# Nine chunks of the batch-weight product as three f16 products, with the splits on Pool

## The chip, the cores and the metric

The kernel runs on one NeuronCore of one Trainium2 chip. The metric is the device time of one execution in microseconds (us); lower is better.

## The reference, cut to what matters

A gated cross-attention block and a gated FFN stand one after the other, on x of 4 batches x 1024 rows x 256 columns, with a context of 154 rows per batch.

```
h   = layernorm(x)                                   # per row of 256
Sim = (h@w1)[:, :, None] + (ctx@w2)[:, None, :] + einsum(h*w3, ctx) + b_sim
A   = softmax(Sim, axis=2);  hq = A @ ctx
hc  = sum_i softmax(max_j Sim)_i * h_i               # one row per batch
out = concat([h, hq, h*hq, h*hc]) @ W_qv + b_qv      # W_qv: 1024 x 256
x1  = x + tanh(g_xattn) * out
y   = layernorm(x1), rounded to 16-bit integers by its largest value
up, gate = y @ Wup.T, y @ Wgate.T                    # 256 -> 768, weights in 4 bits
o   = silu-like product of gate and up, re-rounded at each step by its largest value
result = x1 + tanh(g_ffn) * (o @ Wdown.T)            # 768 -> 256
```

The first and last of the four blocks of `W_qv` are folded: `h @ W0 + (h*hc) @ W3 = h @ (W0 + hc*W3)`. The bracket is the batch weights, `we` in the kernel, one 256x256 matrix per batch. The change is about this product alone.

## The kernel before

The rows are tiled to 16 chunks of 256 (two tiles of 128 rows each), four chunks to a batch: `B = 4`, `NP = 4`, `N = 16`. Every engine has a program of its own, and they meet at semaphores only. In the attention stage each of them runs a loop over a step number `m`, with the order of the work inside a step written out by hand; `b, s = m // NP, m % NP`. Chunk n is normed and turned in step n, scored in step n + 1, and projected in step n + `LAG`, with `LAG = 7`.

On TensorE a step m is: `project(m - 7)`, `turn_h(m)`, `score(m - 1)`, `turn_a(m - 2)`, `attend(m - 3)`, `turn_y(m - 8)`. `project(n)` adds, for each of the two tiles, three pairs of f32 matmuls 128x256 into one PSUM tile: attended rows times W1 (L591), row products times W2 (L593), and rows times batch weights (L597). For the first chunk of a batch the work is parted, since `we` is not there yet: `project_first(b)` does the first two groups (L616, L618) in step 4b + 7, and `project_rest(b)` the third (L628) at that step's end. Between them stand `batch_cols(b)` (L663, L664), which turns the weighted row sum of the batch into a column, and `attend`.

The row sum comes over several engines: DVE's `batch_max` and `batch_shift` and ScalarE's `batch_exp` give a weight per row (`eb`); then Pool's `row_weigh` (L426, L433) and `row_add` (L439 to L443) weigh and sum the rows; `batch_cols` is TensorE's; DVE's `summary` (L1305 to L1313) makes `we` from it.

Pool does, in each step and in this order: `bias_x` for two chunks (in steps with s = 0 or 3; L451), `row_weigh` (s = 1), `y_std(m - 7)` (L397, L399: powers for the second layer norm), `row_add` (s = 2), `row_std(m + 3)` (L392: powers for the first), and parts of the rounding of the FFN weights (L413, L419). In step 16 and 17 the last batch's `row_weigh` and `row_add` come ahead of `y_std`. `row_std` waits for `vp_done`, the end of `stats` on DVE (L1184).

DVE does in step m, as far as it matters here: `attended(m - 4)` (L1231), `norm_x(m + 1)` while m < 7 (L1192), `scored(m - 1)` (L1215), `batch_max`, `stats(m + 3)`, `normed(m - 1)` (L1223), and later `residual(m - 7)` (L1239).

`partition_all_reduce` is a Pool instruction that reduces a column over the 128 partitions. In the kernel before only `over_all` (L488) uses it, four times, in the FFN stage. The projection weights `wv` come in by one DMA (L342) and are used as they are, in f32. The FFN stage follows: `hidden` (L774, L779) makes gate and up, `down` (L809) the last product, both as three f16 products (high x high, high x low, low x high).

Of the kernel before, what the change touches and what calls it, by code (L numbers as in the profile page):

```python
# [62 lines left out]
COLS = 320  # L63
W_SCALE = 2.0 ** 11


def build(nc, x, ctx, g_xattn, g_ffn, w_sim, b_sim, w_qv, b_qv, w_gate, w_up, w_down, out):
# [92 lines left out]
    cx = [cx01[:, 0], cx01[:, 1], cx23[:, 0], cx23[:, 1]]  # L160
    aT = place(a, "aT", [JP, 3, 2, PT], F32)

    a = copy_of(r_wd)
# [31 lines left out]
    c_g3, c_pid = col(3), col()  # L195
    c_bs = c_g3[:, 2:3]
    c_sm, c_sa, c_pw, c_wt, c_dn = col(), col(), col(), col(), col(3)
    c_loc, c_all = col(5), col(5)
# [18 lines left out]
    with ExitStack() as stack:  # L217
        def sem(name):
            return stack.enter_context(nc.semaphore(name))
# [29 lines left out]
        wchain, wall_rdy, wdiag_rdy, wm_ps, wri_rdy, wq_rdy, wqi_rdy, wqf_rdy, wn_rdy, wt_ps, wth_rdy, wt_rdy = map(  # L249
            sem, ("wchain", "wall_rdy", "wdiag_rdy", "wm_ps", "wri_rdy", "wq_rdy", "wqi_rdy", "wqf_rdy", "wn_rdy", "wt_ps", "wth_rdy", "wt_rdy"))  # L250
        ydiag_rdy, ym_ps = sem("ydiag_rdy"), sem("ym_ps")
        l_f_ps, l_xc_rdy, l_x1_rdy, l_bn_done, l_mv_done, l_vp_done, l_rstd_rdy, l_y_rdy, l_yT_ps = map(
# [44 lines left out]
        TURN_AT = {19: (0, 1, 2), 20: (3, 4, 5)}  # L297
        L = N - 1
        w_banks = [hT_bank, s_bank, a_bank]

# [84 lines left out]
        def _(pool):  # L385
# [59 lines left out]
            def bias_x(n):  # L445
# [5 lines left out]
                pool.tensor_tensor(x_, x_, txb[:].unsqueeze(1).broadcast_to([P, 2, D]), ALU.add).then_inc(xb_rdy, 1)  # L451

            pool.wait_ge(mhalf_rdy, 1)
            for n in range(1, NP):
                row_std(n)
            for m in range(N + LAG):
                b, s = m // NP, m % NP
                if s == 3 and 4 <= m < N + 4:
                    for n in range(2):
                        bias_x(m - 5 + n)  # L460
                if s == 0 and 4 <= m < N + 4:
                    for n in range(2):
                        bias_x(m - 4 + n)
                if s == 1 and 1 <= b < B or m == N:
                    row_weigh(b - 1)
                    row_pair(b - 1)
                if m == N + 1:
                    row_add(b - 1)
                for i in range(3):
                    if m == NORMS_AT[i] and i > 0:  # L470
                        weight_n(i)
                if LAG <= m < L + LAG:
                    y_std(m - LAG)
                if s == 2 and 1 <= b < B:
                    row_add(b - 1)
                if 1 <= m and m + 3 < N:
                    row_std(m + 3)
                for i in range(3):
                    if m in (SCALES_AT[i] + 1, SCALES_AT[i] + 2):
                        weight_q(i, m - SCALES_AT[i] - 1)  # L480
                    if m == NORMS_AT[i] and i == 0:
                        weight_n(i)
# [38 lines left out]
        def _(pe):  # L521
# [61 lines left out]
            def project(n, largest_of=None):  # L583
# [3 lines left out]
                for t in range(2):  # L587
# [6 lines left out]
                    if s == 0:  # L594
                        pe.wait_ge(we_rdy, b + 1)
                    for d in range(KD):
                        mm = pe.matmul(o_, hT[:, par, d, q], we[:, par, d, :], start=False, stop=d == KD - 1)  # L597
                    if t == 0 and largest_of is not None:
# [6 lines left out]
            def project_first(b):  # L605
# [3 lines left out]
                if b == 0:  # L609
                    pe.wait_ge(wqv_in, 16)  # L610
                ge(pe, x1_rdy, n - 1)
# [552 lines left out]
        def _(dve):  # L1164
# [68 lines left out]
            def residual(n):  # L1233

                g = 2 * n
                dve.wait_ge(f_ps, n + 1)
                dve.wait_ge(xb_rdy, n + 1)
                x_ = xa[:, g:g + 2, :]
                dve.scalar_tensor_tensor(x_, f_bank[n % 2].rearrange("p (t d) -> p t d", t=2), c_tx, x_,  # L1239
                                         ALU.mult, ALU.add).then_inc(x1_rdy, 1)  # L1240
# [13 lines left out]
            def last_y():  # L1254
# [4 lines left out]
                def last_stats(t):  # L1259
                    x_ = xa[:, 2 * L + t, :]  # L1260
                    dve.wait_ge(l_f_ps, t + 1)
                    i_ = dve.scalar_tensor_tensor(x_, last_f(t), c_tx, x_, ALU.mult, ALU.add)
                    i_.then_inc(l_x1_rdy if t == 0 else x1_rdy, 1)
# [39 lines left out]
            def summary(b):  # L1303
# [6 lines left out]
                if b == 0:  # L1310
                    dve.wait_ge(wqv_in, 16)
                for d in range(KD):
# [27 lines left out]
            def weight_unit(m):  # L1340

                dve.wait_ge(wm_ps, m + 1)
                dve.tensor_reduce(c_sa, s_bank[:, 3 * P:4 * P], AX.X, ALU.max).then_inc(wall_rdy, 1)
                dve.wait_ge(wall_rdy, m + 1)
                ulink(WU * m, dve.tensor_scalar(c_pw.bitcast(I32), c_sa.bitcast(I32), 0x7F800000, None, ALU.bitwise_and))
                ulink(WU * m + 1, dve.reciprocal(c_wt, c_pw))
                dve.tensor_scalar(c_dn[:, m:m + 1], c_pw, 1.0 / W_SCALE, None, ALU.mult)
                ulink(WU * m + 2, dve.tensor_scalar(wsc[:, m % 2], wsc[:, m % 2], c_wt, W_SCALE, ALU.mult, ALU.mult))

# [56 lines left out]
            for m in range(3, N + LAG - 1):  # L1406
# [38 lines left out]
                if s == 3 and b == 1:  # L1445
                    summary(b - 1)
                for i in range(3):
                    if m == SCALES_AT[i]:
# [255 lines left out]
```

## Time and profile before

| | |
|---|---|
| median of 3 runs | 438.53 us (437.5 to 438.99) |
| the profiled execution, its own time | 438.24 us |
| its span in the trace | 436.3 us |
| TensorE (PE) busy | 424.8 us, 97% of the span |
| DVE, ScalarE (ACT), Pool busy | 334.5, 295.3, 120.4 us |
| attention stage | up to about 172 us |
| first matmul of the FFN stage (L774) | 177.51 us |
| granted TensorE clock | 1.00 |

The page's second part shows the span in 40 slices of 10.9 us each, with the busy share in tenths:

```profile
PE   6899999999999999999999999999999999999997
DVE  6885778577573776864446799999899888997784
ACT  4886567568646443943335899994698888977750
POOL 1267545474769541040000213442000000000000
PEclk9999999999999999999999999999999999999999
DMA  7950002000200201100000000000000001343442
```

TensorE is full from about the third slice to the end. From its sixth part, on the projection weights (source, queue, KB, median us from issue to landing):

```profile
wv<-in_L_xattn_W_qv SPq DMA_DIRECT2D x1, 1024.0 KB, 8.2
```

An f32 matmul appears as two records, each with its own weight load. A row of the order of time has start, length, engine, line, operation, output and input; in brackets stands how long the engine had idled before, and who released it.

### The profile page before, as it was taken

The numbers are of one execution on the slowest core, as the hardware profiler recorded it, in microseconds if no ns is written. First come the engines' busy times: TensorE is split into PE (matmuls) and PEld (weight loads), VectorE is DVE, ScalarE is ACT, GpSimd is POOL, SyncE is SP. The second block draws the span as 40 slices with busy tenths as digits, with TensorE's granted clock in tenths as the row PEclk, the third lists the DMA queues.
The fourth block names the chain that finished last, engine by engine and source line by source line (L and its number), as shares of the span: only waits on it lengthen the run. The fifth ranks groups of instructions, "written<-read, shape, count | busy, mean of one in ns | idle before, by whom it ended". The sixth has DMA issues, their size and how long they took to land.

```text
span 436.3 us, 6912 instructions
## 1 busy us (share of the span) xinstructions
PE 424.8 (97%) x2424; PEld 293.6 (67%) x2424; DVE 334.5 (77%) x647; ACT 295.3 (68%) x404; POOL 120.4 (28%) x129
## 2 busy tenths in 40 slices
PE   6899999999999999999999999999999999999997
PEld 5788899999988987444444444444444444888886
DVE  6885778577573776864446799999899888997784
ACT  4886567568646443943335899994698888977750
POOL 1267545474769541040000213442000000000000
PEclk9999999999999999999999999999999999999999
DMA  7950002000200201100000000000000001343442
GB/s 241 326 192 2 1 2 97 2 1 24 75 2 0 98 0 37 61 0 0 0 0 2 0 0 1 0 0 2 0 0 0 0 0 54 116 121 123 144 144 74
DMA packets 20674, 21.14 MB, mean 48 GB/s; under 512 B 826, under 2 KB 20393, under 8 KB 20649
## 3 DMA queue, kind: packets, MB, share of 16 engines
q1 hardware_dynamic: 20628, 20.82, 15.3%
q8 instruction: 14, 0.23, 0.2%
q14 instruction: 12, 0.09, 0.1%
q10 hardware_dynamic: 20, 0.00, 0.0%
HBM read 12.43 MB, written 8.39 MB: 48 GB/s over the span
## 4 chain that ended last, share of the span: by engine, by line
PE 75%; DVE 14%; ACT 6%; issue 4%; POOL 0%; DVEq 0%; ACTq 0%
PE ps L774 17%; PE ps L809 13%; PE ps L779 9%; PE ps L579 5%; PE ps L591 5%; PE ps L597 5%; PE ps L593 5%; DVE cols L1525 5%; PE ps L560 3%; DVE hid L1541 2%; ACT hid L1083 2%; PE ps L569 1%; PE ps L636 1%; PE ps L546 1%; PE ps L628 1%
## 5 line engine op out<-in xcount | busy, mean ns | idle before, releaser
L774 PE MATMUL ps<-xh,wuh 128*128 128x512 f16 x192 | 72.8, 379 | 1.0 <-DVE gq L1565 1.0
L774 PE MATMUL ps<-xh,wul 128*128 128x512 f16 x192 | 72.8, 379 | 0.0
L779 PE MATMUL ps<-xl,wuh 128*128 128x512 f16 x192 | 57.1, 379 | 0.0
L1504 DVE TENSOR_REDUCE cols<-hid x10 | 22.9, 2286 | 24.4 <-ACT hid L1059 24.4
L809 PE MATMUL ps<-wdh,oh 128*128 128x256 f16 x168 | 37.4, 273 | 0.0
L809 PE MATMUL ps<-wdl,oh 128*128 128x256 f16 x168 | 37.4, 273 | 0.0
L1059 ACT ACTIVATE hid<-ps 128x2048 f32 x10 | 18.8, 1875 | 27.5 <-PE ps L779 27.5
L774 PE MATMUL ps<-xh,wgh 128*128 128x512 f16 x96 | 36.4, 379 | 0.1
L774 PE MATMUL ps<-xh,wgl 128*128 128x512 f16 x96 | 36.4, 379 | 0.0
L774 PEld LDWEIGHTS ps<-xh,wuh 128*128 (+1 forms) x192 | 18.8, 98 | 24.3 <-issue 2.0
L779 PEld LDWEIGHTS ps<-xl,wuh 128*128 (+1 forms) x192 | 18.8, 98 | 22.7
L774 PEld LDWEIGHTS ps<-xh,wul 128*128 (+1 forms) x192 | 18.8, 98 | 22.4
L488 POOL PARTITION_ALL_REDUCE cols<-cols x4 | 1.5, 364 | 115.7 <-DVE cols L1463 109.8
L579 PE MATMUL ps<-aT,cx 77*128 77x256 f32 x128 | 30.6, 382 | 0.0
L1146 ACT ACTIVATE oq<-hid,cols 128x1536 int16 (+1 forms) x15 | 23.6, 1572 | 10.1 <-DVE ol L1627 10.1
L921 ACT ACTIVATE yb<-xa,cols 128x256 f32<-128x256 f32 x30 | 16.3, 592 | 20.3 <-POOL cols L399 20.3
L1118 ACT ACTIVATE au<-ps,cols 128x512 int16<-128x512 f32 x40 | 25.8, 691 | 5.6 <-PE ps L779 5.6
L1541 DVE CUSTOM_DVE_ANT_0 hid<-ag,sq 128x2048 f32<-128x2048 int16 x12 | 29.1, 2424 | 0.2
L1525 DVE TENSOR_REDUCE cols<-ps 128x1 f32<-128x2048 f32 x12 | 27.4, 2285 | 1.6 <-PE ps L779 1.6
L779 PE MATMUL ps<-xl,wgh 128*128 128x512 f16 x96 | 28.6, 379 | 0.0
L591 PE MATMUL ps<-wv,hqT 128*128 128x256 f32 x104 | 26.7, 379 | 0.0
L597 PE MATMUL ps<-we,hT 128*128 128x256 f32 x104 | 26.7, 379 | 0.0
(235 smaller groups left out, 1025.7 us busy)
## 6 DMA issues: line engine op xcount, KB each, us to landing
x_scratch<-xa SPq DMA_DIRECT2D x4, 1024.0 KB, 4.4
xo<-x_scratch SPq DMA_DIRECT2D x16, 256.0 KB, 2.9
out_dram<-xo SPq DMA_DIRECT2D x15, 256.0 KB, 2.6
xa<-in_x SPq DMA_DIRECT2D x3, 1024.0 KB, 12.6
xa<-in_x SPq DMA_DIRECT2D x4, 256.0 KB, 4.5
wv<-in_L_xattn_W_qv SPq DMA_DIRECT2D x1, 1024.0 KB, 8.2
wr<-in_L_ffn_w_gate SPq DMA_DIRECT2D x1, 768.0 KB, 10.1
wr<-in_L_ffn_w_up SPq DMA_DIRECT2D x1, 768.0 KB, 11.5
```

The costliest lines, as they stand in the source:

```text
L579: mm = pe.matmul(hq_bank[:, d * PT:(d + 1) * PT], cx[b][0:JP, k, d * P:(d + 1) * P], aT[0:JP, n % 3, k, :], start=k == 0, stop=k == 1)
L591: pe.matmul(o_, hqT[:, par, d, q], wv[:, KD + d, :], start=d == 0, stop=False)
L593: pe.matmul(o_, prT[:, par, d, q], wv[:, 2 * KD + d, :], start=False, stop=False)
L597: mm = pe.matmul(o_, hT[:, par, d, q], we[:, par, d, :], start=False, stop=d == KD - 1)
L774: pe.matmul(ps[hf][:, q, :], w_[:, d, ds(k * P, P)], xh[:, d, n], start=d == 0 and w_ is wh, stop=False)
L779: mm = pe.matmul(ps[hf][:, q, :], wh[:, d, ds(k * P, P)], xl[:, d, n], start=False, stop=d == KD - 1)
L809: mm = pe.matmul(down_ps(par)[:, t], o_[:, par, k, q], w_[:, k, :], start=not low and k == 0 and w_ is wdh, stop=low and k == KF - 1)
L1118: a_ = act.activation(au[:, hf, bank_of(q)], ps[hf][:, q, :], ACT.Abs, scale=c_cu)
L1146: act.activation(oq[:, par], hid[:, :, ds(c * CD, CD)], ACT.Copy, scale=c_co).then_inc(oqa_rdy, 1)
L1504: dve.tensor_reduce(gmx[:, ds(k * 2 + hf, 1)], unit(hid, k, hf), AX.X, ALU.max, apply_absolute_value=True).then_inc(gm_done, 1)
L1525: dve.tensor_reduce(umx[:, u:u + 1], ps_half(u % 2), AX.X, ALU.max, apply_absolute_value=True).then_inc(half_free[u % 2], 1)
L1541: dve.tensor_tensor_reduce(half_of(hid, u), ag[:, u % 2, :], sq[u % 2][:], 1.0, 0.0, ALU.mult, ALU.max, pmx[:, u:u + 1]).then_inc(p_rdy, 1)
```

## The change

For the nine chunks 1, 2, 3, 5, 6, 7, 9, 10 and 11 (`SPLIT`) the group of L597 is no longer two f32 matmuls a tile but six f16 matmuls: high rows x high weights, high x low, low x high, for each of the two halves of the contraction. The chunks 0, 4, 8 (`project_rest`) and the last batch stay in f32.

Pool makes the f16 parts: `split_h(i)` casts the turned rows of a chunk to f16 and subtracts the cast from them, at the start of step n + 6; `split_weights(b)` does the same for `we`, in the steps with s = 3.

For the low parts to stay in f16's range, the projection weights are first scaled by a power of two: at step 3 DVE takes their largest absolute value per partition (`all_weights_largest`), at step 4 Pool reduces it over the partitions (`all_weights_max`, a `partition_all_reduce`) and DVE makes the scale and its inverse (`all_weights_unit`), at step 5 Pool multiplies all 128x2048 values in place (`all_weights_scaled`). The semaphore counts of another chain of DVE move by one set of three for it. What used `wv` waits for the scaling: `project_first(0)` and `summary(0)`. The residual takes the gate times the inverse scale (`c_txs`) in place of the gate (`c_tx`). The f16 tiles lie in memory that the FFN's up weights take later.

```diff
--- before.py
+++ after.py
@@ -62,6 +62,7 @@
 LN_EPS = 1e-5
 COLS = 320
 W_SCALE = 2.0 ** 11
+V_SCALE = 2.0 ** 10


 def build(nc, x, ctx, g_xattn, g_ffn, w_sim, b_sim, w_qv, b_qv, w_gate, w_up, w_down, out):
@@ -159,6 +160,11 @@
     cx23 = place(copy_of(r_wg), "cx23", [JP, 2, 2, D], F32)
     cx = [cx01[:, 0], cx01[:, 1], cx23[:, 0], cx23[:, 1]]
     aT = place(a, "aT", [JP, 3, 2, PT], F32)
+    a = copy_of(r_wu)
+    hTh = place(a, "hTh", [P, 2, KD, PT], F16)
+    hTl = place(a, "hTl", [P, 2, KD, PT], F16)
+    weh = place(a, "weh", [P, KD, D], F16)
+    wel = place(a, "wel", [P, KD, D], F16)

     a = copy_of(r_wd)
     cbi = place(a, "cbi", [P, 2, J], F32)
...
@@ -296,6 +304,7 @@
         TURNS = [(0, 0), (0, 1), (0, 2), (1, 0), (1, 1), (1, 2), (2, 0), (2, 1), (2, 2)]
         TURN_AT = {19: (0, 1, 2), 20: (3, 4, 5)}
         L = N - 1
+        SPLIT = [n for n in range(N - NP) if n % NP > 0]
         w_banks = [hT_bank, s_bank, a_bank]

         def w_part(m, q, low):
@@ -450,11 +459,47 @@
                 x_ = xa[:, 2 * n:2 * n + 2, :]
                 pool.tensor_tensor(x_, x_, txb[:].unsqueeze(1).broadcast_to([P, 2, D]), ALU.add).then_inc(xb_rdy, 1)

+            def split_h(i):
+
+                n = SPLIT[i]
+                b, s, par = place_of(n)
+                pool.wait_ge(pr_rdy, n + 1)
+                if i > 1:
+                    pool.wait_ge(f_ps, SPLIT[i - 2] + 1)
+                seen = hT[:, par, :, s * PT:(s + 1) * PT]
+                pool.tensor_copy(hTh[:, i % 2], seen).then_inc(hhl_rdy, 1)
+                pool.wait_ge(hhl_rdy, 2 * i + 1)
+                pool.tensor_tensor(hTl[:, i % 2], seen, hTh[:, i % 2], ALU.subtract).then_inc(hhl_rdy, 1)
+
+            def split_weights(b):
+
+                pool.wait_ge(we_rdy, b + 1)
+                ge(pool, f_ps, b * NP)
+                pool.tensor_copy(weh[:], we[:, b % 2]).then_inc(wvs_rdy, 1)
+                pool.wait_ge(wvs_rdy, 2 * b + 3)
+                pool.tensor_tensor(wel[:], we[:, b % 2], weh[:], ALU.subtract).then_inc(wvs_rdy, 1)
+
+            def all_weights_max():
+
+                pool.wait_ge(vunit_rdy, 1)
+                pool.partition_all_reduce(c_va, c_vg, P, RMAX).then_inc(wvs_rdy, 1)
+
+            def all_weights_scaled():
+
+                pool.wait_ge(vunit_rdy, 3)
+                pool.tensor_scalar(wv[:], wv[:], c_vs, 1.0, ALU.mult, ALU.mult).then_inc(wvs_rdy, 1)
+
             pool.wait_ge(mhalf_rdy, 1)
             for n in range(1, NP):
                 row_std(n)
             for m in range(N + LAG):
                 b, s = m // NP, m % NP
+                if m - LAG + 1 in SPLIT:
+                    split_h(SPLIT.index(m - LAG + 1))
+                if m == 5:
+                    all_weights_scaled()
+                if s == 3 and LAG <= m < N:
+                    split_weights(b - 1)
                 if s == 3 and 4 <= m < N + 4:
                     for n in range(2):
                         bias_x(m - 5 + n)
@@ -475,6 +520,8 @@
                     row_add(b - 1)
                 if 1 <= m and m + 3 < N:
                     row_std(m + 3)
+                if m == 4:
+                    all_weights_max()
                 for i in range(3):
                     if m in (SCALES_AT[i] + 1, SCALES_AT[i] + 2):
                         weight_q(i, m - SCALES_AT[i] - 1)
@@ -593,8 +640,18 @@
                         pe.matmul(o_, prT[:, par, d, q], wv[:, 2 * KD + d, :], start=False, stop=False)
                     if s == 0:
                         pe.wait_ge(we_rdy, b + 1)
-                    for d in range(KD):
-                        mm = pe.matmul(o_, hT[:, par, d, q], we[:, par, d, :], start=False, stop=d == KD - 1)
+                    if n in SPLIT:
+                        i = SPLIT.index(n)
+                        pe.wait_ge(hhl_rdy, 2 * i + 2)
+                        pe.wait_ge(wvs_rdy, 2 * b + 4)
+                        for d in range(KD):
+                            qt = slice(t * P, (t + 1) * P)
+                            pe.matmul(o_, hTh[:, i % 2, d, qt], weh[:, d, :], start=False, stop=False)
+                            pe.matmul(o_, hTh[:, i % 2, d, qt], wel[:, d, :], start=False, stop=False)
+                            mm = pe.matmul(o_, hTl[:, i % 2, d, qt], weh[:, d, :], start=False, stop=d == KD - 1)
+                    else:
+                        for d in range(KD):
+                            mm = pe.matmul(o_, hT[:, par, d, q], we[:, par, d, :], start=False, stop=d == KD - 1)
                     if t == 0 and largest_of is not None:
                         batch_max(largest_of)
                     if n == L:
@@ -607,7 +664,7 @@
                 n, par = b * NP, b % 2
                 pe.wait_ge(pr_rdy, n + 1)
                 if b == 0:
-                    pe.wait_ge(wqv_in, 16)
+                    pe.wait_ge(wvs_rdy, 2)
                 ge(pe, x1_rdy, n - 1)
                 for t in range(2):
                     q = slice(t * P, (t + 1) * P)
@@ -1235,8 +1292,10 @@
                 g = 2 * n
                 dve.wait_ge(f_ps, n + 1)
                 dve.wait_ge(xb_rdy, n + 1)
+                if n == 0:
+                    dve.wait_ge(vunit_rdy, 3)
                 x_ = xa[:, g:g + 2, :]
-                dve.scalar_tensor_tensor(x_, f_bank[n % 2].rearrange("p (t d) -> p t d", t=2), c_tx, x_,
+                dve.scalar_tensor_tensor(x_, f_bank[n % 2].rearrange("p (t d) -> p t d", t=2), c_txs, x_,
                                          ALU.mult, ALU.add).then_inc(x1_rdy, 1)
                 dve.wait_ge(x1_rdy, n + 1)
                 for t in range(2):
@@ -1259,7 +1318,7 @@
                 def last_stats(t):
                     x_ = xa[:, 2 * L + t, :]
                     dve.wait_ge(l_f_ps, t + 1)
-                    i_ = dve.scalar_tensor_tensor(x_, last_f(t), c_tx, x_, ALU.mult, ALU.add)
+                    i_ = dve.scalar_tensor_tensor(x_, last_f(t), c_txs, x_, ALU.mult, ALU.add)
                     i_.then_inc(l_x1_rdy if t == 0 else x1_rdy, 1)
                     dve.wait_ge(l_x1_rdy if t == 0 else x1_rdy, 1 if t == 0 else N)
                     dve.bn_stats(st[:, t, :], x_).then_inc(l_bn_done, 1)
@@ -1308,7 +1367,7 @@
                 dve.wait_ge(hc_rdy, b + 1)
                 ge(dve, f_ps, NP * (b - 1))
                 if b == 0:
-                    dve.wait_ge(wqv_in, 16)
+                    dve.wait_ge(wvs_rdy, 2)
                 for d in range(KD):
                     i_ = dve.scalar_tensor_tensor(we[:, b % 2, d, :], wv[:, 3 * KD + d, :], c_hc[:, d:d + 1], wv[:, d, :],
                                                   ALU.mult, ALU.add)
@@ -1342,10 +1401,24 @@
                 dve.wait_ge(wm_ps, m + 1)
                 dve.tensor_reduce(c_sa, s_bank[:, 3 * P:4 * P], AX.X, ALU.max).then_inc(wall_rdy, 1)
                 dve.wait_ge(wall_rdy, m + 1)
...
+
+            def all_weights_largest():
+
+                dve.wait_ge(wqv_in, 16)
+                ulink(0, dve.tensor_reduce(c_vl, wv[:].rearrange("p k n -> p (k n)"), AX.X, ALU.max, apply_absolute_value=True))
+                dve.tensor_scalar(c_vg, c_vl, EPS, None, ALU.max).then_inc(vunit_rdy, 1)
+
+            def all_weights_unit():
+
+                dve.wait_ge(wvs_rdy, 1)
+                ulink(1, dve.tensor_scalar(c_vp.bitcast(I32), c_va.bitcast(I32), 0x7F800000, None, ALU.bitwise_and))
+                ulink(2, dve.reciprocal(c_vi, c_vp))
+                dve.tensor_scalar(c_vs, c_vi, V_SCALE, None, ALU.mult).then_inc(vunit_rdy, 1)
+                dve.tensor_scalar(c_txs, c_vp, c_tx, 1.0 / V_SCALE, ALU.mult, ALU.mult).then_inc(vunit_rdy, 1)

             def weight_values(m):
@@ -1444,6 +1517,10 @@
                     batch_shift(b - 1)
                 if s == 3 and b == 1:
                     summary(b - 1)
+                if m == 3:
+                    all_weights_largest()
+                if m == 4:
+                    all_weights_unit()
                 for i in range(3):
                     if m == SCALES_AT[i]:
                         weight_scales(i)
```

## Rows read from the trace of the kernel before

**Rows 1.** Stages: us; PE, PEld, DVE, ACT, POOL busy; clock; DMA share, GB/s
```profile
20.00:40.00 20.00, 19.48 (x125) 17.61 (x123) 15.33 (x62) 16.06 (x47) 14.72 (x16) 1.00 0.43 127
60.00:80.00 20.00, 20.00 (x121) 18.09 (x119) 16.57 (x56) 15.41 (x40) 13.57 (x17) 1.00 0.16 54
```

**Rows 2.** TensorE in order of time, steps 6 and 7
```profile
28.08 0.60 PE L546 MATMUL ps<-ident,h 128*128 128x128 f32 x4
...
31.78 1.03 PE L616 MATMUL ps<-wv,hqT 128*128 128x256 f32 x4
...
37.83 0.61 PE L663 MATMUL ps<-ones,h 128*128 128x1 f32 x4 [0.20 <-POOL h L443]
...
41.62 1.99 PE L628 MATMUL ps<-we,hT 128*128 128x256 f32 x8 [0.60 <-DVE we L1313]
```

**Rows 3.** TensorE in order of time: groups of one projection
```profile
63.96 1.03 PE L597 MATMUL ps<-we,hT 128*128 128x256 f32 x4
64.82 1.03 PE L591 MATMUL ps<-wv,hqT 128*128 128x256 f32 x4
```

**Rows 4.** TensorE in order of time: f16 matmuls of the down projection
```profile
420.31 1.36 PE L809 MATMUL ps<-wdh,ol 128*128 128x256 f16 x11
```

**Rows 5.** DVE and the queue of SyncE in order of time
```profile
3.21 0.47 SPq L342 DMA_DIRECT2D wv<-in_L_xattn_W_qv  x1
...
20.96 0.69 DVE L1231 TENSOR_TENSOR prT<-hqT,hT 128x512 f32<-128x512 f32 x1
...
24.56 0.18 DVE L1184 TENSOR_SCALAR cols<-cols 128x2 f32<-128x2 f32 x1
...
24.73 0.67 DVE L1231 TENSOR_TENSOR prT<-hqT,hT 128x512 f32<-128x512 f32 x1
25.31 0.72 DVE L1192 TENSOR_SCALAR h<-xa,cols 128x256 f32<-128x256 f32 x2
```

**Rows 6.** The page's groups: busy, mean ns of one, idle before and its releaser
```profile
L1525 DVE TENSOR_REDUCE cols<-ps 128x1 f32<-128x2048 f32 x12 | 27.4, 2285 | 1.6 <-PE ps L779 1.6
```

**Rows 7.** Pool in order of time, steps 4 to 6
```profile
24.82 1.26 POOL L392 TENSOR_TENSOR cols<-cols 128x2 f32<-128x2 f32 x1
29.88 2.00 POOL L426 TENSOR_SCALAR h<-h,cols 128x256 f32<-128x256 f32 x4 [3.81 <-ACT cols L971]
...
37.05 0.73 POOL L443 TENSOR_TENSOR h<-h 128x256 f32<-128x256 f32 x1
```

**Rows 8.** Pool's reductions: its queue's instructions by line, and order of time
```profile
L488 POOLq MODIFY_POOL_CONFIG  x2: 11/11/11, 300.8 to 300.8; - x2
...
305.17 0.17 DVE L1463 TENSOR_REDUCE cols<-cols 128x1 f32<-128x12 f32 x1
...
306.58 0.38 POOL L488 PARTITION_ALL_REDUCE cols<-cols  x1 [6.00 <-issue]
...
240.91 0.38 POOL L488 PARTITION_ALL_REDUCE cols<-cols  x1 [49.15 <-DVE cols L1463]
...
L492 POOLq MODIFY_POOL_CONFIG  x2: 83/83/83, 241.2 to 241.3; - x2
...
241.78 0.21 DVE L1516 TENSOR_SCALAR cols<-cols 128x1 f32<-128x1 f32 x1
...
248.09 2.30 POOL L492 TENSOR_SCALAR gq<-hid,cols 128x2048 int16<-128x2048 f32 x1 [6.80 <-issue]
```

**Rows 9.** Lines L503 and L507: ns min/median/max of one
```profile
L503 POOL CAST wdh<-wdt x3: 609/609/613, 186.6 to 187.7; 128x512 f16<-128x512 f32 x3
...
L507 POOL TENSOR_TENSOR wdl<-wdt,wdh x3: 1156/1160/1164, 188.4 to 190.6; 128x512 f16<-128x512 f32 x3
```

**Rows 10.** Pool and TensorE in order of time, steps 15 to 18
```profile
123.18 1.07 POOL L397 TENSOR_TENSOR cols<-cols 128x2 f32<-128x2 f32 x1 [5.54 <-DVE cols L1252]
...
137.95 0.73 POOL L443 TENSOR_TENSOR h<-h 128x256 f32<-128x256 f32 x1
...
142.99 0.50 PE L663 MATMUL ps<-ones,h 128*128 128x1 f32 x4
```

More of the change, by code:

```diff
@@ L196, in build @@
     c_bs = c_g3[:, 2:3]
+    c_vl, c_vg, c_va, c_vp, c_vi, c_vs, c_txs = (col() for _ in range(7))
     c_sm, c_sa, c_pw, c_wt, c_dn = col(), col(), col(), col(), col(3)
@@ L250, in build @@
             sem, ("wchain", "wall_rdy", "wdiag_rdy", "wm_ps", "wri_rdy", "wq_rdy", "wqi_rdy", "wqf_rdy", "wn_rdy", "wt_ps", "wth_rdy", "wt_rdy"))
+        vunit_rdy, wvs_rdy, hhl_rdy = map(sem, ("vunit_rdy", "wvs_rdy", "hhl_rdy"))
         ydiag_rdy, ym_ps = sem("ydiag_rdy"), sem("ym_ps")
@@ L1344, in weight_unit @@
                 dve.wait_ge(wall_rdy, m + 1)
-                ulink(WU * m, dve.tensor_scalar(c_pw.bitcast(I32), c_sa.bitcast(I32), 0x7F800000, None, ALU.bitwise_and))
-                ulink(WU * m + 1, dve.reciprocal(c_wt, c_pw))
+                ulink(WU * (m + 1), dve.tensor_scalar(c_pw.bitcast(I32), c_sa.bitcast(I32), 0x7F800000, None, ALU.bitwise_and))
+                ulink(WU * (m + 1) + 1, dve.reciprocal(c_wt, c_pw))
                 dve.tensor_scalar(c_dn[:, m:m + 1], c_pw, 1.0 / W_SCALE, None, ALU.mult)
-                ulink(WU * m + 2, dve.tensor_scalar(wsc[:, m % 2], wsc[:, m % 2], c_wt, W_SCALE, ALU.mult, ALU.mult))
+                ulink(WU * (m + 1) + 2, dve.tensor_scalar(wsc[:, m % 2], wsc[:, m % 2], c_wt, W_SCALE, ALU.mult, ALU.mult))
+            def all_weights_largest():
[8 more added lines that the diff above has]
+                dve.tensor_scalar(c_txs, c_vp, c_tx, 1.0 / V_SCALE, ALU.mult, ALU.mult).then_inc(vunit_rdy, 1)
             def weight_values(m):
```

## The prediction

> **What bounds the kernel now.** I read the table of stages first. In the attention stage (the first 172 of 436.3 us) TensorE is busy 19.48 of 20 us between 20 and 40 us and all of the 20 us between 60 and 80 us, at granted clock 1.00, while Pool has 5 us and DVE 3 us or more to spare [rows 1]. So from about 43 us on, a microsecond of TensorE work taken out is a microsecond of the end, and what another engine is late is lost when TensorE stands. Second, TensorE in order of time, steps 6 and 7 of the loop over m [rows 2]. Before `project_first(0)` at 31.78 the steps hold no projection and are short. Two of the gaps name the neighbours: `batch_cols(0)` (L663) at 37.83 waited 0.20 us for Pool's last row sum (L443), and `project_rest(0)` (L628) at 41.62 waited 0.60 us for DVE's batch weights. The reader is to see that Pool's chain to L443 already ends last there: there is no slack for it to be late in.
>
> **TensorE's gain.** A group `rows x batch weights` (L597) of one 128-row tile is two f32 matmuls, four records; it starts at 63.96 and the next group at 64.82, so it costs 0.865 us [rows 3]. The new group is six f16 matmuls 128x256. The down projection runs just these: in its 11 records of 1.36 us, the last one's 0.27 us taken off, ten starts take 1.09 us, 0.109 us each [rows 4]. Six are 0.654 us, the gain 0.21 us a tile. `SPLIT` is chunks 1, 2, 3, 5, 6, 7, 9, 10, 11: nine chunks, 18 tiles, 18 x 0.21 = **-3.8 us**. All of it is on the path. Were the mix with f32 neighbours to cost one more start each, 2 us would be left; nothing in the rows gives more than 3.8.
>
> **DVE's new work at m = 3.** `all_weights_largest` is a reduction over 128x2048 f32; one of that size takes 2.285 us on DVE [rows 6], with its small maximum about 2.45 us. The projection weights are long there (its DMA was issued at 3.21 us and landed 8.2 us later, by the page's last part), so it starts when `stats(6)` is through, at 20.96, where `attended(0)` starts now [rows 5]. Behind it stand, in order, `attended(0)`, `norm_x(5)`, `scored(3)` and `stats(7)`: all 2.45 us later. `h(6)`, which step 5 makes, is ready at 25.31 + 0.72 = 26.03 and TensorE turns it at 28.08 [rows 2, 5]: 2.0 us of slack there, and none that I see on the way to Pool.
>
> **The reduction over partitions at m = 4.** This is where I expect the time to go. Pool does `row_std(7)` first, which waits for `stats(7)`: now it follows L1184 of 24.56 and lasts from 24.82 to 26.08 [rows 5, 7]; 2.45 us later is 28.5. Then comes `partition_all_reduce`. What such an instruction costs among ordinary Pool work is shown late in the trace: after the last L498 Pool's queue issues MODIFY_POOL_CONFIG at 300.8; the number to be reduced was written by DVE at 305.17 + 0.17 = 305.34, and the reduction starts only at 306.58, 1.2 us after its input and 5.8 us after the configuration. Back it is the same: MODIFY_POOL_CONFIG at 241.2, the last scale that L492 needs at 241.78 + 0.21 = 241.99, and L492 starts at 248.09, 6.9 us after the configuration, with 6.80 us of idle time put down to issue [rows 8]. The reduction itself is 0.38 us. Each way was mostly hidden in the FFN stage, since Pool has nothing else to do; at m = 4 it has. I take both as measured.
>
> - Reduction starts at 28.5 + 5.8 = 34.3, ends at 34.7.
> - DVE waits for it at the end of its step 4 (`all_weights_unit`). Then four dependent small instructions of about 0.2 us, 0.9 us: DVE begins step 5 at 35.6, where it began at 24.73 [rows 5]: 10.9 us later. Queued behind that wait: `attended(1)`, `norm_x(6)`, `scored(4)`, so the turns and scores of TensorE's step 6.
> - Pool's configuration goes back from 34.3 + 0.3 = 34.6 and the next ordinary instruction starts at 34.6 + 6.9 = 41.5. That is `all_weights_scaled` over 128x2048, as long as L492 on the same size, 2.30 us [rows 8]: done at 43.8. `project_first(0)` and DVE's `summary(0)` now wait for it. TensorE wanted it at 31.78 [rows 2]: 12.0 us later.
> - Behind it on Pool are `row_weigh(0)`, `row_pair`, `row_std(8)` and `row_add(0)`, which now run from 29.88 to 37.05 + 0.73 = 37.78 without a gap, 7.9 us [rows 7]. New: 43.8 + 7.9 = 51.7, **13.9 us later**. TensorE, 12.0 us late, would be at `batch_cols(0)` at 49.6 and waits 2.1 us. So Pool's chain decides.
> - Given back: `project_rest(0)` stood 0.60 us for DVE after `batch_cols(0)`, as DVE was then still in its own step; after such a long stall it is not. 13.9 - 0.6 = **+13.3 us**.
>
> Nothing makes this up later: TensorE is full from 43 us on [rows 1], so a shift there is a shift of the end. Bounds of the term: 4.6 us if both switches were free (first rival), and about 19 us if a switch in the midst of the input loads takes half as long again; I stay with the measured 5.8 and 6.9. TensorE stands some 5 us around 32 to 37 us; the granted clock is 1.00 in all stages shown, and if it fell to half (1.2 GHz), the four groups of `project_first(0)` (3.46 us) could double and come 1.4 us after Pool's chain. I hold that in the range, not in the sum.
>
> One rule bears on the sum. The Trainium skill (GPSIMD Engine Reference, section 2.1 Instruction dispatch) says that the first call into a freshly loaded Pool kernel also pays for loading its code, about 6 us (5.95 us measured). By it both ways would be 11.9 us in place of my 12.7, and the end 0.8 us earlier; the rows above go a little past it on the way back, and I keep the rows.
>
> **Pool's splits.** A cast of 128x512 is 0.609 us, the subtraction 1.160 us [rows 9]; with the wait between them 1.85 us for a chunk and as much for a batch's weights: 12 x 1.85 = 22 us on an engine that has 6 to 8 us free in each 20. Most of it falls into Pool's waits for `vp2`, one in most steps (5.54 us in the first of rows 10). The weights' split (m = 7, 11, 15) starts at `we_rdy`; between that and its use by L597 TensorE does at least `project_rest` and two groups, 4 x 0.865 = 3.5 us [rows 3], against 1.85: nothing. In steps 15 to 17 Pool runs without a gap from `y_std(8)` at 123.18 to L443 at 137.95 + 0.73 = 138.68, and TensorE's `batch_cols(3)` is at 142.99 [rows 10]: 4.3 us of slack. Two splits go into that chain (+3.7 us) and three shortened projections bring TensorE there 1.3 us sooner: 0.7 us too late. **+0.7 us**, bounds 0 and 3. The reuse waits of the f16 tiles (`f_ps` of two splits before) are met by then; the residual only takes another column.
>
> **Sum.** 438.24 (the profiled execution; span 436.3) - 3.8 + 13.3 + 0.7 = 448.4. The median of the three runs is 0.3 us above that execution, within their spread. I predict 448.5 us, about 2.3% slower.
>
> **Rivals.**
> 1. *The switches cost nothing here* (Pool's reduction comes as promptly as when it was long prepared). Reduction at 28.6, DVE back at 29.9, 5.2 us late; the exponentials of batch 0 and with them Pool's row sums 5.2 us late, 0.6 given back: +4.6 + 0.7 - 3.8 = 439.7. For it: the round trip is short when the configuration was made early. Against: the configuration needs Pool, which is at work until 28.5. 8%.
> 2. *Faster*: the reduction, the switches and the scaling all fall into slack before TensorE fills up at 43 us, and the shorter products decide: 438.24 - 3.8 + 0.7 = 435.1. It decides if the stall of DVE at m = 4 is below about 2 us (the slack of `h(6)`). Against: L663 already waits for Pool. 3%.
> 3. *The first switch is longer*, since the input loads run into the third slice of the page (21.8 to 32.7 us) and the code must come over the same engines: half as long again both ways, +6 us: 454.5. 9%.
> 4. *Pool becomes the bound in general* by its 22 us and holds TensorE in each step: another 3 us or more over my forecast, 452 and up. For it: the dense chain in steps 15 to 17. Against: 5 to 6 us of wait in most other steps. 7%.
>
> My forecast has 73%, with 446 to 451 as its own range. The range for 8 in 10: 443.5 (a shorter switch, or one partly hidden) to 453.5. A measurement of this kernel tells 0.3% (1.3 us) from no change: slower 0.91 (forecast, rivals 3 and 4, and part of 1), within it 0.05, faster 0.04.
>
> **What would show it.** Right: MODIFY_POOL_CONFIG on Pool's queue near 28 and 34.5 us and Pool idle for about 6 us after each; a DVE wait of 6 to 7 us on Pool at m = 4; L663 of batch 0 near 51 to 52 us, released by Pool; then 0.42 us less in each of nine steps; the first FFN matmul near 187.7 us instead of 177.5. Wrong: the reduction within 1 us of `row_std(7)`, or `project_first(0)` before 38 us; six f16 matmuls taking over 0.75 us; further TensorE waits on `hhl_rdy`.

## The result, and the profile after

| | before | after |
|---|---|---|
| median of six runs each | 438.44 us | 453.18 us |
| lowest, highest | 437.5, 438.99 | 451.63, 454.75 |
| profiled execution, its span | 438.24, 436.3 | 451.92, 450.1 |
| mean granted clock | 1.0 | 0.981 |

The ratio is 1.0337, interval 1.0317 to 1.0357: 3.4% slower. The median lies 0.3 us inside the range for 8 in 10 (443.5 to 453.5) and above the forecast's own (446 to 451); no run stands near it, three of after are at 451.6 to 452.1 and three at 454.2 to 454.8.

The page of after. Line numbers are 9 higher in Pool's part than before, 47 to 57 in TensorE's, 57 in ScalarE's and 57 to 59 in those of DVE shown here.

```profile
span 450.1 us, 7047 instructions
PE 428.6 (95%) x2460; PEld 293.7 (65%) x2460; DVE 345.7 (77%) x653; ACT 294.9 (66%) x404; POOL 141.8 (32%) x155
PE   6875999999999979999999999999999999999997
POOL 1322896689589954112000013344000000000000
PEclk9976899999999999999999999999999999999999
```

TensorE is short of work in the third and fourth slice (22 to 45 us), and its clock falls there; Pool is busy 141.8 us, where it was busy 120.4. First Pool in order of time, which answers to [rows 7, 8] (start us, us, engine, line, operation, and in brackets the idle time before it and what ended it):

```profile
34.70 0.38 POOL L485 PARTITION_ALL_REDUCE cols<-cols  x1 [5.96 <-issue]
42.31 1.96 POOL L490 TENSOR_SCALAR wv<-wv,cols 128x2048 f32<-128x2048 f32 x1 [7.23 <-issue]
...
51.23 0.73 POOL L452 TENSOR_TENSOR h<-h 128x256 f32<-128x256 f32 x1
```

The two switches are there, both put down to issue, that is to nothing that the profile shows. The rows of the source lines L485 and L490 show when Pool's queue asked for each (first and last start), and who waited:

```profile
L485 POOLq MODIFY_POOL_CONFIG  x2: 11/11/11, 28.9 to 29.0; - x2
...
  DVE cols L1418: 7.1, 1
...
L490 POOLq MODIFY_POOL_CONFIG  x2: 83/83/83, 35.0 to 35.1; - x2
```

From 28.9 to 34.70 it is 5.8 us, from 35.0 to 42.31 it is 7.3. DVE stood for it, with everything of its steps 5 and 6 behind (these rows answer to [rows 5]):

```profile
21.02 2.28 DVE L1412 TENSOR_REDUCE cols<-wv 128x1 f32<-128x2048 f32 x1
...
35.11 0.15 DVE L1418 TENSOR_SCALAR cols<-cols 128x1 int32<-128x1 int32 x1 [7.08 <-POOL cols L485]
```

And TensorE, which answers to [rows 2 to 4] (`project_first` is now L673, `batch_cols` L720, the f16 products L649 to L651):

```profile
37.07 1.11 PE L593 MATMUL ps<-ident,h 128*128 128x128 f32 x4 [3.24 <-DVE h L1249]
...
44.41 2.05 PE L673 MATMUL ps<-wv,hqT 128*128 128x256 f32 x4 [1.69 <-POOL wv L490]
...
52.02 0.61 PE L720 MATMUL ps<-ones,h 128*128 128x1 f32 x4
...
56.99 1.03 PE L638 MATMUL ps<-wv,hqT 128*128 128x256 f32 x4
...
58.72 0.27 PE L649 MATMUL ps<-weh,hTh 128*128 128x256 f16 x1
...
59.37 0.81 PE L638 MATMUL ps<-wv,hqT 128*128 128x256 f32 x3
```

`batch_cols(0)` is at 52.02, where it was at 37.83: 14.2 us late. What follows `project_rest(0)` starts at 56.99, where it started at 43.45: 13.5 late. Six f16 matmuls take 59.37 - 58.72 = 0.65 us in place of 0.865.

The late part is in order of time too, TensorE first:

```profile
145.20 0.60 PE L616 MATMUL ps<-ident,sc 128*77 128x128 f32 x4
...
148.51 0.66 PE L693 MATMUL ps<-ident,yb 128*128 128x128 f32 x4 [0.98 <-ACT yb L978]
...
154.00 0.59 PE L720 MATMUL ps<-ones,h 128*128 128x1 f32 x4
...
159.55 1.13 PE L654 MATMUL ps<-we,hT 128*128 128x256 f32 x4 [0.73 <-DVE we L1372]
...
164.91 0.66 PE L693 MATMUL ps<-ident,yb 128*128 128x128 f32 x4 [1.65 <-ACT yb L978]
...
191.47 0.39 PE L831 MATMUL ps<-xh,wgh 128*128 128x512 f16 x1
```

None of the three bracketed waits was there before. The ends of matmuls are modelled, so I count from start to start: by that these three places are 1.1, 0.9 and 1.8 us longer than before. At 145.20 the kernel is 10.2 us behind (before, the same turn was at 134.98): 13.5 less eight chunks at 0.42 us. At the first matmul of the FFN (191.47, before 177.51) it is 14.0 us behind, though one more chunk was split (9.8 expected). So the late waits cost 4.2 us. From there to the end both kernels take the same (258.6 and 258.8 us). The whole account of the spans: +13.5 - 3.8 + 4.2 - 0.1 = +13.8.

Where the last two of the late waits come from is on DVE and on Pool, in the same view of after, DVE first:

```profile
155.31 4.18 DVE L1372 SCALAR_TENSOR_TENSOR we<-wv,cols 128x256 f32<-128x256 f32 x2
```
```profile
153.21 0.73 POOL L452 TENSOR_TENSOR h<-h 128x256 f32<-128x256 f32 x1
...
156.25 2.96 POOL L428 TENSOR_TENSOR wr<-wr,wsc 128x1536 f32<-128x1536 f32 x1
```

DVE's two instructions for the last batch's weights took 0.88 us before (at 144.22); here they take 4.18, and the row of the line gives 2.992 us as its longest and 0.497 as its median. They end at 155.31 + 4.18 = 159.49, just after Pool's product over 128x1536 (156.25 + 2.96 = 159.21). The first of the two took 1.2 us (the second starts at 156.5): it stood beside the Pool instruction ahead of that product, which ended at 156.29. Before, Pool's product was through when they began, and 0.4 us ahead of them:

```profile
141.00 2.78 POOL L419 TENSOR_TENSOR wr<-wr,wsc 128x1536 f32<-128x1536 f32 x1
```

### The profile page after: what moved, and what is told of

Same layout as the page of the kernel before. It is cut to its first block, busy times and chain, and to the rows that moved or that the text cites. A ratio compares the mean times of both kernels' runs of the same rounds, so it can differ in the third digit from the quotient of the medians.

```text
span 450.1 us, 7047 instructions
## 1 busy us (share of the span) xinstructions
PE 428.6 (95%) x2460; PEld 293.7 (65%) x2460; DVE 345.7 (77%) x653; ACT 294.9 (66%) x404; POOL 141.8 (32%) x155
## 3 DMA queue, kind: packets, MB, share of 16 engines
q1 hardware_dynamic: 20628, 20.82, 14.7%
## 4 chain that ended last, share of the span: by engine, by line
PE 63%; DVE 14%; issue 7%; POOL 6%; ACT 5%; DMA 2%; SPq 1%; DVEq 0%; POOLq 0%; ACTq 0%
PE ps L831 17%; PE ps L866 12%; PE ps L836 8%; DVE cols L1602 4%; PE ps L638 3%; PE ps L640 3%; PE ps L626 3%; DMA xa<-in_x 2%; DVE hid L1618 2%; PE ps L607 2%; ACT hid L1140 2%; ACT ag L1145 1%; POOL h L435 1%; PE ps L904 1%; PE ps L693 1%
## 5 line engine op out<-in xcount | busy, mean ns | idle before, releaser
L626 PE MATMUL ps<-aT,cx 77*128 77x256 f32 x128 | 32.3, 398 | 0.0
L640 PE MATMUL ps<-wv,prT 128*128 128x256 f32 x104 | 26.7, 379 | 0.0
```

The lines of the kernel that those rows point to most:

```text
L626: mm = pe.matmul(hq_bank[:, d * PT:(d + 1) * PT], cx[b][0:JP, k, d * P:(d + 1) * P], aT[0:JP, n % 3, k, :], start=k == 0, stop=k == 1)
L640: pe.matmul(o_, prT[:, par, d, q], wv[:, 2 * KD + d, :], start=False, stop=False)
```

## The experiments

All ten stand against runs of the kernel before on the same chip (medians 438.38 to 438.49). Times are medians. The fences show the main lines of each edit; `...` stands for what is left out.

**e1, without the reduction over partitions.** An ordinary sum of two columns takes its place; the maximum over partitions is left out, so the power of two is each partition's own, and the kernel no longer computes the reference's result. It serves for the time alone.

```
- pool.partition_all_reduce(c_va, c_vg, P, RMAX).then_inc(wvs_rdy, 1)
+ pool.tensor_tensor(c_va, c_vg, c_vg, ALU.add).then_inc(wvs_rdy, 1)
```

> The changed kernel with the reduction over partitions replaced by a sum of the column with itself on Pool: the maximum over the partitions is left out, and with it both code switches of Pool; DVE's reduction, its wait for Pool, the small instructions and the scaling of all weights stay. Theory (the two switches of 5.8 and 6.9 us are what costs): the early loss falls from 13.5 us to about 4.6 us, so 453.2 - 8.9 = 444 us (442 to 446). Rival (the work itself, DVE's 2.3 us reduction and the added instructions and waits, costs): stays above 450 us.

Measured: 443.76 us, ratio 1.011 (1.0083 to 1.0137); 9.4 us below after, where the theory had 8.9. The scaling starts at once, and `batch_cols(0)` is 8.4 us earlier:

```profile
29.99 2.34 POOL L490 TENSOR_SCALAR wv<-wv,cols 128x2048 f32<-128x2048 f32 x1 [0.81 <-DVE cols L1421]
...
43.66 0.61 PE L720 MATMUL ps<-ones,h 128*128 128x1 f32 x4 [0.20 <-POOL h L452]
```

**e2, without the scaling.** Reduction, unit and `all_weights_scaled` are gone and the residual takes `c_tx` again; nine chunks are still three f16 products.

```
- if m == 5:
-     all_weights_scaled()
...
- if m == 4:
-     all_weights_max()
...
- if m == 3:
-     all_weights_largest()
- if m == 4:
-     all_weights_unit()
```

> The changed kernel without the scaling of the projection weights (no largest value, no reduction, no unit, no multiplication; V_SCALE gone); the splits and the f16 products stay. Theory: the early loss is gone whole, -3.8 us of products and 0.7 to 4.2 us of late losses are left: 435.3 to 438.8 us, so the same as before or up to 0.7% faster. Rival (Pool's 22 us of splits hold TensorE in every step): above 442 us.

Measured: 437.78 us, ratio 0.999 (0.9976 to 1.0004). The splits alone thus gain nothing that can be told from zero, though 3.8 us of TensorE work is gone: the three late waits stay, at 0.99, 0.73 and 1.65 us. DVE's pair beside Pool's long product is as long as in after:

```profile
141.15 4.18 DVE L1366 SCALAR_TENSOR_TENSOR we<-wv,cols 128x256 f32<-128x256 f32 x2
```

**e3, the scaling alone.**

```
- SPLIT = [n for n in range(N - NP) if n % NP > 0]
+ SPLIT = []
...
- if s == 3 and LAG <= m < N:
-     split_weights(b - 1)
```

> The changed kernel with SPLIT empty and no split of the weights: the scaling alone, all products in f32. Theory: only the early loss of 13.5 us, no late loss: 438.4 + 13.5 = 452 us. Rival (early stall partly caused by the splits queued behind it, or given back): below 448 us.

Measured: 453.45 us, ratio 1.0341 (1.0308 to 1.0374). TensorE has no late wait between 100 and 170 us. With e2 the parts add up: +15.1 and -0.6 make +14.5, and after is +14.7. It is 1.5 us over the theory. A part of that is the wait of `project_rest(0)` for DVE's batch weights, which the prediction had given back: it is still there with the scaling alone, and gone with the splits alone (e3 first, then e2):

```profile
56.53 1.99 PE L683 MATMUL ps<-we,hT 128*128 128x256 f32 x8 [0.61 <-DVE we L1370]
```
```profile
40.97 1.99 PE L681 MATMUL ps<-we,hT 128*128 128x256 f32 x8
```

**e4, a reduction that nobody reads.** The kernel before, with one more Pool instruction; the lines without a plus are there already.

```
  if 1 <= m and m + 3 < N:
      row_std(m + 3)
+ if m == 4:
+     pool.partition_all_reduce(c_va, mhalf[:, 0:1], P, RMAX)
```

> The kernel before with one reduction over partitions added on Pool after row_std of step 4, whose result nobody reads or waits for. It measures the two switches on Pool alone. Theory (Pool's own chain to the batch row sum decides): Pool is away from 26.1 us for 5.8 + 0.3 + 6.9 us, the row sums start at about 39.1 instead of 29.9 us, 0.6 given back: 438.4 + 8.6 = 447 us (445 to 449). Rival (it is DVE's wait for the result that costs, Pool's absence is hidden): 438 to 440 us.

Measured: 450.51 us, ratio 1.0269 (1.0223 to 1.0315): 12.1 us for a reduction of 0.38 us and no data. The rival, that Pool's absence is hidden (438 to 440), falls, and the theory is 3.5 us short. Pool pays both switches, and TensorE waits 9.53 us in one piece:

```profile
32.79 0.38 POOL L480 PARTITION_ALL_REDUCE cols<-cols  x1 [6.46 <-issue]
40.09 1.83 POOL L427 TENSOR_SCALAR h<-h,cols 128x256 f32<-128x256 f32 x4 [6.93 <-issue]
...
47.41 1.01 PE L666 MATMUL ps<-ones,h 128*128 128x1 f32 x4 [9.53 <-POOL h L444]
...
48.71 3.76 PE L582 MATMUL ps<-aT,cx 77*128 77x256 f32 x8
```

That last row's work took 1.97 us before. The table of stages (length, busy time of PE, PEld, DVE, ACT, POOL, granted clock, DMA share, GB/s) shows a full TensorE at half clock after the wait:

```profile
45.00:50.00 5.00, 2.59 (x9) 2.41 (x10) 3.42 (x14) 1.97 (x6) 4.84 (x6) 0.50 0.00 0
50.00:55.00 5.00, 5.00 (x14) 4.11 (x14) 1.15 (x2) 2.07 (x6) 0.47 (x1) 0.50 0.02 3
55.00:60.00 5.00, 5.00 (x23) 4.37 (x22) 2.94 (x10) 0.13 (x1) 1.43 (x3) 0.95 0.00 0
```

**e8, the same with TensorE kept at work.** It is e4 with 18 f32 matmuls that nobody reads, ahead of TensorE's wait for Pool.

```
  def batch_cols(b):
+     if b == 0:
+         pe.wait_ge(txb_rdy, 1)
+         for i in range(18):
+             pe.matmul(f_bank[1][:, 0:D], ident[:], wv[:, i % 8, :], start=True, stop=True)
      pe.wait_ge(hs_rdy, b + 1)
```

> The kernel with the lone reduction (e4), and 18 f32 matmuls 128x256 (ident times wv, into a PSUM tile that is unused then; about 7.8 us) on TensorE ahead of its wait for the row sum of batch 0. Theory (the 9.5 us stall is followed by some 9 us at granted clock 0.50, which costs what the stall alone does not explain): the clock stays at 1.00 and 450.5 falls by about 2.7 us to 447.8 us. Rival (the rest of the loss is in the lengths of the code switches or in Pool): 450.5 us.

Measured: 448.28 us, ratio 1.0231 (1.0202 to 1.0259), 2.2 us below e4. The two intervals overlap and each has four runs only, so the times alone do not settle it; the traces do. From `batch_cols(0)` to the first product of the next step it is 5.62 us in the kernel before (37.83 to 43.45), 8.71 in e4 (47.41 to 56.12) and 6.58 in e8 (47.27 to 53.85). What follows the wait is at full speed again at first, though the clock still dips for a while after it:

```profile
47.27 0.60 PE L670 MATMUL ps<-ones,h 128*128 128x1 f32 x4 [1.14 <-POOL h L444]
...
50.00:55.00 5.00, 5.00 (x18) 4.03 (x18) 1.71 (x3) 2.00 (x5) 0.52 (x1) 0.67 0.00 0
```

So in e4 Pool's chain comes 9.6 us late, and 3.1 more are lost behind it with TensorE at the lower clock, as an effect of the wait: with TensorE kept at work 2.1 of them are back.

**e5, the normalised weights one step later**, without the scaling (as e2), so that Pool's long product stands elsewhere.

```
- NORMS_AT = [12, 18, 20]
+ NORMS_AT = [12, 19, 20]
```

> The kernel without scaling (e2), with Pool's weight_n(1) (a product of 128x1536, 2.95 us) in step 19 instead of 18. Theory (DVE's batch weights of the last batch are stretched from 0.88 to 4.18 us because Pool's product runs at the same time, and the waits of TensorE for we and for the turned y of chunk 11 follow from it): that instruction pair is back near 1 us, 0.73 + 1.65 us of TensorE's waits go, 437.8 - 2.4 = 435.4 us. Rival (Pool is merely late by its splits, whatever it runs beside): 437.8 us as before.

Measured: 436.32 us, ratio 0.9948 (0.993 to 0.9966). DVE's pair falls from 4.18 to 1.66 us and the 0.73 us wait is gone, but the time is 0.9 us over the theory. The wait of 0.99 us stays, from Pool's late chain (it is gone in e6). One of 0.43 us is new in its place, at 156.33, and comes of the move: Pool's product now runs from 151.23 to 154.00, and a DVE instruction over 128x2 beside it, which took 0.17 us at that place before, takes 1.53 (152.50 to 154.03). The second layer norm waits for it.

**e6, seven splits**, without the scaling: chunks 10 and 11 stay f32. **e10** is the same kernel again, timed beside e9.

```
- SPLIT = [n for n in range(N - NP) if n % NP > 0]
+ SPLIT = [n for n in range(N - NP) if n % NP > 0 and n < 10]
```

> The kernel without scaling (e2), with seven chunks split instead of nine (10 and 11 stay in f32). Theory (the late losses come from the two splits in Pool's gapless steps 16 and 17): 7 x 0.42 = 2.9 us gained and no late loss, 438.4 - 2.9 = 435.5 us. Rival (each chunk's gain is lost in its own step): 437.8 us or slower.

> The seven-chunk kernel (e6) once more, beside e9 on one chip, to compare them: 435.4 us, 0.8 us above e9 by the theory of e9 (two chunks less, 2 x 0.42 us).

Measured: 435.43 us, ratio 0.9934 (0.991 to 0.9958), and 434.93, ratio 0.9917 (0.9904 to 0.9931). No late wait is left, and DVE's pair takes 1.26 us:

```profile
140.98 1.26 DVE L1366 SCALAR_TENSOR_TENSOR we<-wv,cols 128x256 f32<-128x256 f32 x2
```

Two splits fewer are 0.84 us more TensorE work, and the kernel is 2.3 us faster than e2. The last two splits cost more than they save, by Pool's time. This kernel and e9 are the fastest of the study, 0.7% to 0.8% ahead of the kernel before.

**e7, the cast on ScalarE**, without the scaling, all nine chunks: Pool only subtracts.

```
- pool.tensor_copy(hTh[:, i % 2], seen).then_inc(hhl_rdy, 1)
...
+ act.activation(hTh[:, i % 2], hT[:, par, :, s * PT:(s + 1) * PT], ACT.Copy).then_inc(vunit_rdy, 1)
```

> The kernel without scaling (e2), with the cast of each chunk's rows on ScalarE at the end of step n + 5; Pool only subtracts (1.16 us a chunk instead of 1.85). Theory: the row sum of the last batch comes about 1.4 us earlier on Pool and weight_n(1) with it, so it overlaps DVE's batch weights less; 435.5 to 437 us. Rival (ScalarE's 0.6 us a step delays its own chain and TensorE waits for it): above 438 us.

Measured: 437.04 us, ratio 0.9969 (0.9956 to 0.9981). Pool's chain is shorter and the first late wait falls from 0.99 to 0.29 us, but its long product still meets DVE's weights (3.60 us for the pair), and the 1.65 us wait stays. The rival's wait is there as well: at 108.83 TensorE stands 0.62 us for a DVE instruction (L1274), as it does in no kernel without the casts on ScalarE.

**e9, e7's cast and e5's step.**

> The kernel without scaling (e2) with both remedies: the casts of the rows on ScalarE (as e7) and weight_n(1) in step 19 (as e5); all nine chunks split. Theory (nothing but Pool's 0.69 us casts in its gapless steps and its long product beside DVE's batch weights takes the gain back): the waits of 0.99 and 1.65 us for the turned y and the 0.73 us for we are gone or below 0.5 us together, so the whole 3.8 us are left: 434.6 us (434 to 435.5). Rival (ScalarE's added casts make a wait of their own, as the 0.6 us in e7): 436 us or more.

Measured: 435.06 us, ratio 0.992 (0.9906 to 0.9933). Of the late waits 0.29 and 0.20 us are left; the 0.20 has the same cause as the 0.43 in e5 (DVE's 128x2 instruction takes 1.53 us beside Pool's moved product). The rival's wait is there too, 0.65 us at 110.26, so it holds in part. I expected 0.8 us below e10 and found 0.1 above: the two are not told apart. The trace of e9 is of its slowest run (437.61 us), which is 1.7 us behind e10's by the time of `batch_cols(0)`.

## Why the prediction was right, and which term was not

**The early term, predicted +13.3, measured +13.5.** DVE's reduction took 2.28 us at 21.02 (predicted 2.45 in all at 20.96). The way to the reduction is 5.8 us as predicted, and the way back 7.3 against 6.9; `batch_cols(0)` came at 52.02 against 51.7. The signs given for it were there: the configurations asked for at 28.9 and 35.0 (near 28 and 34.5 forecast), DVE's wait of 7.1 us on Pool (6 to 7). e4 shows that the reduction's place between ordinary Pool work is enough for 12.1 us, e1 that 9.4 us come back when the reduction alone goes, while the rest of the scaling (DVE's reduction, Pool's 2 us over 128x2048 ahead of its chain) is worth 443.76 - 437.78 = 6.0 us (rival 1 had 5.2 for that stall). The Trainium skill (GPSIMD Engine Reference, section 2.1 Instruction dispatch) has about 6 us for the first call into a freshly loaded kernel. Both ways agree with it in the order of size; what passes in them no row shows. The way back, to ordinary arithmetic, is the longer one each time: 7.3 us against 5.8 in after, 7.0 against 6.4 in e4, 6.9 against 5.8 late in the kernel before.

**The 0.6 us given back came by luck.** The prediction says that after so long a stall DVE would be through with its own step. In e3, with about the same stall, TensorE waits those 0.61 us all the same, and in e2, with no stall, it does not. What differs is Pool. In the kernel before, `bias_x` runs beside DVE's last small instruction of `stats`, ahead of the batch weights in DVE's order:

```profile
38.40 2.49 POOL L451 TENSOR_TENSOR xa<-xa,txb 128x512 f32<-128x512 f32 x2
...
38.78 0.91 DVE L1184 TENSOR_SCALAR cols<-cols 128x2 f32<-128x2 f32 x1
```

It takes 0.83 us in e3, where `bias_x` is beside it too. With the splits, `split_h` and `split_weights` stand ahead of `bias_x`, and the same instruction takes 0.25 us in e2 and 0.17 in after:

```profile
53.06 0.17 DVE L1241 TENSOR_SCALAR cols<-cols 128x2 f32<-128x2 f32 x1
```

So the 0.6 us belong to the splits, which the forecast had at nothing here, and not to the stall.

**One step was off, and it cancelled.** I had TensorE wait 2.1 us for Pool at `batch_cols(0)`. It has no wait there that the profile counts: its last matmul ahead of it starts at 51.32 and Pool's sum ends at 51.97, so the two come within a few tenths of a microsecond. It was slow itself, since the clock had fallen, which I had held possible in the range. The clock fell twice. The first time was at 27 us (0.56 from 27 to 28 us), after a wait of 1.7 us that ended at 25.59. It was at 1.00 again from 41 to 44 us and fell anew as TensorE took up work after the wait of 1.69 us for the scaled weights (0.59, 0.50, 0.50 and 0.70 in the four microseconds from 44 us). There `project_first(0)` took 5.1 us in place of 3.46. The table of stages of after:

```profile
25.00:30.00 5.00, 3.56 (x18) 2.97 (x19) 2.88 (x15) 2.62 (x8) 0.70 (x1) 0.71 0.76 271
30.00:35.00 5.00, 3.83 (x10) 2.57 (x9) 0.00 (x0) 0.59 (x1) 0.30 (x1) 0.50 0.01 2
35.00:40.00 5.00, 2.93 (x12) 2.94 (x13) 4.69 (x21) 2.45 (x10) 0.07 (x1) 0.50 0.00 0
40.00:45.00 5.00, 3.31 (x15) 2.69 (x15) 3.04 (x12) 4.45 (x13) 2.69 (x2) 0.84 0.00 0
```

0.50 is the 1.2 GHz level, 1.00 the one of 2.4 GHz. Pool's chain was still the longer one, by those few tenths, so the clock cost next to nothing in after. In e4, where TensorE's long wait came right ahead of full work, it cost 3.1 us by the trace. A stall has two prices, and the second depends on what stands behind it.

**TensorE's gain, predicted -3.8.** 0.65 us a tile against 0.865 in the rows, 0.42 us a chunk down to 145.20. Right.

**The late term, predicted +0.7 with bounds 0 and 3, measured +4.2.** This is the mis-sized one, and 3.5 of the 4.7 us by which the median lies over the forecast; with it the first FFN matmul came at 191.47 and not near 187.7 us. I priced the two splits in Pool's steps 15 to 17 by when the row sum for `batch_cols(3)` is ready. That place costs nothing: it starts as Pool's last sum ends (153.21 + 0.73 = 153.94, and 154.00), since TensorE had lost 1.1 us at the turned y a step earlier. What I left out is all else that the same chain feeds: `y_std`, on which ScalarE and the turned y wait (0.98 us), and the place of the next long Pool instruction. It slid onto DVE's batch weights and made 0.88 us into 4.18; the products wait for them (0.73 us), then the turned y (1.65 us). e2 has all three waits without the scaling, e3 none without the splits. The stretch was also the one with the least room on Pool: in the kernel before it was busy 16.2 of the 20 us from 120 to 140, so 3.8 us were free and not the 6 to 8 of the forecast. e5 moves the product, and of the last two waits (2.4 us) one of 0.4 us elsewhere is left; e6 leaves out the last two splits, and all three are gone.

**What is left of the error.** The median is 1.3 us over the profiled execution (451.92), which is itself 3.5 over the forecast's 448.4. The whole account of terms is that of one execution, of the lower of the two groups of runs. What parts the groups by 2 to 3 us no experiment asked, and it stays open; had all six fallen into the upper one, the time would have lain outside the range. To that extent the range held by luck.

**The rivals.** Free switches (439.7) fall by e4 and by the rows; so does the faster case. Longer switches (454.5) are near the median in number, but not in kind: they are 5.8 and 7.3 us, and not half as long again. Pool as the bound in general (452 and up) is the closest: it does hold TensorE, but only around the last batch's row sum and with 4.2 us, not in each step (at 145.20, after eight of the nine splits, nothing of their gain was lost).

## What to carry to other kernels

Before one instruction of another kind goes onto Pool, look in the trace for how long Pool stands around such an instruction elsewhere, on the way back as well as there, and look for a place where Pool has nothing else to do (no run here moved the reduction to one). When work is added to Pool, follow everything that its chain feeds, and ask beside which instructions of DVE its long ones will now stand; e5 shows that a product moved away from one can land on another. TensorE work moved onto Pool pays only where Pool has gaps: seven splits of nine gain 0.7% to 0.8%, all nine, with Pool as it is, nothing; with the cast on ScalarE and the long product moved (e9), nine gain the same.

## What was not expected of the hardware

- DVE's `scalar_tensor_tensor` on two f32 inputs of 128x256 took 2.99 us in place of 0.48 beside a Pool product over 128x1536, and ended 0.3 us after it. The Trainium skill (SBUF — State Buffer, section "SBUF: two separate sides") has a DVE instruction with two SBUF inputs and a Pool instruction hold a shared pair of ports one at a time, the one that comes second blocked for the whole of the other. The row agrees in that DVE was through only after Pool.
- DVE's `TENSOR_SCALAR` over 128x2, 0.17 us alone, took 0.91 beside `bias_x` in the kernel before and 1.53 beside the product over 128x1536 in e5, where it ended at 154.03 and the product at 154.00.
- A reduction of 0.38 us that nobody reads made the kernel 12.1 us longer; by the trace some 3 of them were TensorE's clock after a wait of 9.5 us.
- The way to the reduction took 5.8 us both at 28.9 us in after and late in the kernel before. In after the input loads were nearly through by then (DMA share 0.62 from 28 to 29 us, 0.21 in the next). In e4 and e8 it was asked for at 26.4 and 26.9 us, with the DMA share at 0.93 and 1.03 in that microsecond, and took 6.4 and 5.5 us: one a little longer, one a little shorter, and no more can be said.
